# Edge attention: VectorE's one-hots and scalings take their second operand from PSUM instead of SBUF

## The reference, cut to what matters

```python
e = attn_src[:, src_idx] + attn_dst[:, dst_idx]
e = jnp.where(e >= 0, e, NEG_SLOPE * e)
e = e * edge_weight[None, :]
e_exp = jnp.exp(e - jnp.max(e))
denom = jax.ops.segment_sum(e_exp.T, dst_idx, num_segments=num_nodes).T
alpha = e_exp / (denom[:, dst_idx] + 1e-10)
msg = h[:, src_idx] * alpha[..., None]
out = jax.vmap(lambda m: jax.ops.segment_sum(m, dst_idx, num_segments=num_nodes))(msg)
```

## Time and profile before

| | us |
|---|---|
| median of 3 runs | 5927.24 |
| lowest and highest | 5904.29, 5947.91 |
| profiled execution, span | 5765.0 |
| TensorE, busy | 4607.2 (80%) |
| VectorE, busy | 2716.3 (47%) |
| ScalarE, busy | 2120.2 (37%) |
| GpSimd, busy | 836.5 (15%) |
| mean granted clock of TensorE | 0.885 |

### The profile page before, as it was taken

The page is one execution under the profiler, slowest core; times in us unless marked ns, Lnnn a source line. Parts: engine busy times, 40 slices in busy tenths (PEclk is TensorE's granted clock), DMA queues, the critical chain, the costliest instruction groups (busy, mean ns, idle before and its releaser), DMA issues. The chain is left out here.

```text
span 5765.0 us, 88635 instructions
## 1 busy us (share of the span) xinstructions
PE 4607.2 (80%) x24482; PEld 3873.4 (67%) x24483; DVE 2716.3 (47%) x5068; ACT 2120.2 (37%) x3279; POOL 836.5 (15%) x769
## 2 busy tenths in 40 slices
PE   3888868888856499669589989899769959969666
PEld 2677645555545399438578778788659959969555
DVE  5555567777653400321379689689631140020233
ACT  2333215544433200424256566566524420020332
POOL 2778710000005200002100000000022200000000
PEclk8788889999968799789799999999779979989878
DMA  3433311211113342113211111111122134224000
GB/s 97 113 111 106 101 37 71 79 71 75 66 62 100 106 161 109 30 34 116 65 51 56 46 44 55 42 49 55 39 71 97 36 93 162 109 92 159 36 17 24
DMA packets 150165, 438.52 MB, mean 76 GB/s; under 512 B 25592, under 2 KB 89805, under 8 KB 133676
## 3 DMA queue, kind: packets, MB, share of 16 engines
q1 hardware_dynamic: 115212, 341.23, 16.7%
q0 software_dynamic: 34848, 96.08, 5.9%
HBM read 340.98 MB, written 96.25 MB: 76 GB/s over the span
## 5 line engine op out<-in xcount | busy, mean ns | idle before, releaser
L2404 PE MATMUL p_acc<-p_H,p_eT 125*125 125x256 f32 x3750 | 823.5, 378 | 0.0
L2404 PEld LDWEIGHTS p_acc<-p_H,p_eT 125*125 125x125 f32 x3750 | 695.2, 187 | 106.0
L1033 POOL DMA_INDIRECT p_message<-edge_table,p_index x425 | 503.8, 1185 | 131.2 <-issue 120.9
L1951 DVE TENSOR_REDUCE p_mean<-F 128x1 f32<-128x3125 f32 x10 | 34.0, 3403 | 931.7 <-PEq L83 931.7
L1246 PE MATMUL p_acc<-p_message,p_spread 125*125 125x260 f32 x1666 | 425.6, 422 | 28.7 <-issue 28.7
L1298 POOL IOTA p_order_i<- 125x200 int32 x3 | 1.1, 381 | 2882.6 <-SPq L81 2882.6
L1705 ACT ACTIVATE p_hid<-p_up,p_b1s 128x125 f32<-128x125 f32 x764 | 273.0, 366 | 395.6 <-PE p_up L1681 352.5
L1246 PEld LDWEIGHTS p_acc<-p_message,p_spread 125*125 125x125 f32 x1666 | 348.4, 211 | 98.1 <-issue 30.6
L1681 PEld LDWEIGHTS p_up<-p_xT,p_w1s 128*128 128x128 f32 x3056 | 377.8, 199 | 51.3 <-issue 33.1
L1681 PE MATMUL p_up<-p_xT,p_w1s 128*128 128x125 f32 x3056 | 385.5, 283 | 32.9 <-issue 11.8
L835 PE MATMUL p_acc<-p_cell,p_heavy 125*125 (+1 forms) x1440 | 405.4, 392 | 0.0
(11 more groups left out here) (441 smaller groups left out, 8080.0 us busy)
## 6 DMA issues: line engine op xcount, KB each, us to landing
sums_first<-edge_sums SPq DMA_DIRECT2D x48, 1250.0 KB
p_second<-edge_sums SPq DMA_DIRECT2D x48, 1250.0 KB, 6.7
p_count<-edge_counts SPq DMA_DIRECT2D x75, 762.9 KB
edge_sums<-p_sums SPq DMA_DIRECT2D x32, 1250.0 KB, 4.4
edge_counts<-p_total SPq DMA_DIRECT2D x32, 610.4 KB
p_w1s<-in_L_ffn_W SPq DMA_DIRECT2D x16, 1024.0 KB
p_got<-made SPq DMA_DIRECT2D x25, 560.0 KB
p_dst_all<-dst_row SPq DMA_DIRECT2D x25, 531.2 KB
```

Of the source, the lines that this page charges most:

```text
L1033: pool.indirect_dma_start(message[:, m, k, :], None, table, bass.IndirectOffsetOnAxis(ap=index[:, m, k:k + 1], axis=0)).then_inc(landed[m] ...
L1951: then(dve.tensor_reduce(mean[:, h:h + 1], F[:, h], AX_X, ALU.add))
L2404: last = pe.matmul(acc[:, s, 0:C], eT[:, r % 4, a % 4], H[:, a, 0:C], start=(a == 0), stop=(a == T - 1))
```

## The change

Two tensors are added in PSUM. `dst_of` is a copy of `g.dstf` (443 columns), made once by ScalarE at the start. `power` holds the exponentials, 4 for each chunk; ScalarE writes them there by a second ACTIVATE in front of the one that writes them into `message` (TensorE still multiplies those columns, so that one stays). The comparison in `spreads` reads `dst_of` for `g.dstf`, and the product in `scales` reads `power` for the last columns of `message`. The wait in `scales` asks for both ACTIVATEs.

```diff
+        dst_of = ph.psum("dst_of", [P, 512])
+        power = ph.psum("power", [P, SETS, R_CH, HEADS])
+        dst_kept = ph.sem("dst_kept")
...
             def exponents(r, m):
                 act.wait_ge(logit_ready, r + 1)
+                act.activation(power[:, m], logit[:], ACT.Exp, bias=minus[:, m:m + 1]).then_inc(raised, 1)
                 act.activation(message[0:P, m, :, C:W], logit[:], ACT.Exp, bias=minus[:, m:m + 1]).then_inc(raised, 1)
...
             for m in range(SETS):
                 indices(m, m)
+            act.activation(dst_of[:, 0:CH + PAD], g.dstf[:], ACT.Copy).then_inc(dst_kept, 1)
             act.wait_ge(setup, 2)
...
                     dve.tensor_tensor(spread[:, lo:lo + n], g.iota[:, nodes(t)].unsqueeze(1).to_broadcast([P, n, P]),
-                                      g.dstf[:, bass.ds(r * R_CH + lo, n)].unsqueeze(2).to_broadcast([P, n, P]),
+                                      dst_of[:, bass.ds(r * R_CH + lo, n)].unsqueeze(2).to_broadcast([P, n, P]),
                                       ALU.is_equal).then_inc(spread_ready, 1)
...
-                dve.wait_ge(raised, r + 1)
+                dve.wait_ge(raised, 2 * r + 2)
                 for lo, n in PIECES:
                     rows_of = message[0:P, m, lo:lo + n]
                     o = rows_of[:, :, 0:C].rearrange("p k (h o) -> p k h o", h=HEADS)
-                    dve.tensor_tensor(o, o, rows_of[:, :, C:W].unsqueeze(3).to_broadcast([P, n, HEADS, HO]), ALU.mult).then_inc(scaled, 1)
+                    dve.tensor_tensor(o, o, power[:, m, lo:lo + n].unsqueeze(3).to_broadcast([P, n, HEADS, HO]), ALU.mult).then_inc(scaled, 1)
...
             (first, _, _), = g.tiles_of(nc, DVE, 0)
+            dve.wait_ge(dst_kept, 1)
             spreads(0, first, 0)
```

## The result

| | before | after |
|---|---|---|
| median, us | 5937.57 (4 runs) | 6128.39 (4 runs) |
| lowest and highest | 5904.29, 5955.75 | 6123.31, 6131.05 |
| profiled execution, span | 5765.0 | 6127.9 (timed at 6129.59) |

The ratio is 1.030, 95% interval 1.027 to 1.034: slower by 191 us, where 42 us less were forecast.

A forecast was written before the change was run, and what follows sets the result against it. GpSimd's gathers were taken to set the pace, 25.4 us a round, with TensorE's chain next at 23.4. Waits of 36.4 + 5.5 = 42 us go, added work costs 0: 5927 to 5885 us, range 5843 to 5935.

The forecast's parts named there:

- Gathers lose their stretch: GpSimd's 425 gathers beside one-hots and scalings: their stretch goes entirely, taking 102 us off GpSimd.
- The row it rested on: Line 1758 in another stage, one operand in PSUM: the gather beside it took 0.97 us; all six such pairs read so.
- The second operand in PSUM costs nothing: One-hots and scalings on VectorE: reading one operand from PSUM was taken as 0, with a lower bound of -11 ns an instruction.
- the rest of what was added: Second ACTIVATE, scalings' wait for two, later factors and the copy: hidden beside other work, cost 0; uncovered, the ACTIVATE costs 8.8 us.
- rival with a dear broadcast operand: One-hots and scalings cost more with a PSUM broadcast operand, VectorE becomes the bound: 5923 if doubled, 5993 at 2.5; chance 0.06.
- What of it reaches the end: Edge-attention stage: of 102 us off GpSimd only what TensorE now waits is gained, 42 us.
- the sum of the waits: Per round the smaller of VectorE's landing wait and TensorE's transpose wait: 36.4 us in rounds 3 to 24, plus 5.5 us.
- Does a new wait take their place? ... I count nothing: Refilled gathers land just in time behind a one-visit round, with 8 us to spare behind two; counted as nothing.
- TensorE's chain of 23.4 us: A two-visit round without gather waits: visits 17.47, terms 3.4, transpose to next visit 2.5 us; the next bound.
- The 162 us between span and median: Difference between the profiled span of 5765 and the median of 5927; expected to stay unchanged.
- The range: Whole-kernel median expected between 5843 and 5935 us, forecast plus runs' spread, third case and no effect partly included.
- the one rival on the slow side: Same as the rival with a dear broadcast operand: VectorE becomes the bound; chance 0.06.

The follow-up runs named there:

- extras only: The change with both operands read from SBUF again, all added work kept: 5747 us, 0.997 in one session; 5938 us, 1.000 in another.
- first chip: The chip of set 1, on which the kernel before took 5758 us; on the other four it took 5865 to 5938 us.
- Each half: Against the kernel before, only the one-hots (5718 us, 0.992) or only the scalings (5717 us, 0.992) read their second operand from PSUM.
- set 3: Another chip, against before: extras only 1.000, one-hots alone from PSUM 1.031, scalings alone from PSUM 1.001, before with a register load behind each gather 1.012.
- set 5: GpSimd waits for the new maximum: the change, before all 17 gathers 1.018, behind the first five 0.998; kernel before, behind the first five 0.989.
- sets 2 to 4: Runs on three other chips: the change again, register loads, halves, added comparisons behind the one-hots and 80-byte gathers; ratios to before from 1.000 to 1.041.
- paced kernels: A GpSimd register load added behind each gather: on the change 6011 us, 1.022; on the kernel before 5999 us, 1.012.
- held kernel: One-hots alone from PSUM, plus an unread comparison with both operands in SBUF behind each one-hot piece: 6031 us, 1.028.
- set 1: One chip: kernel before unchanged 5757 us, 1.000; extras only 0.997; one-hots alone from PSUM 0.992; scalings alone from PSUM 0.992.
- set 2: Another chip: kernel before unchanged 5862 us; the change again 6097 us, 1.038; the change with a register load behind each gather 6011 us, 1.022.

## Why the prediction was wrong, point by point

- **Gathers lose their stretch: right.** Forecast 950 ns, measured 946; 119 gathers ran beside the two lines, all at 0.95 us. The two lines are its cause: 1052 with the one, 1066 with the other. The row it rested on has more like it than was said: 46 gathers of that stage, and not six, overlap an instruction of line 1758; 45 took 0.97 or 0.98 us, one 1.08.
- **The second operand in PSUM costs nothing: right,** and so did the rest of what was added (extras only: 0.997 and 1.000). The rival with a dear broadcast operand fell: 1215 against 1217 ns.
- **What of it reaches the end: right only on the first chip.** Each half gave 40 us there, where I had put 42 for both, so the sum of the waits was hit by luck or was too small; the two together were not run there. The scalings' half gives nothing on the chip of set 3.
- **"Does a new wait take their place? ... I count nothing": this step failed.** I asked only whether the rows would land in time, and took TensorE's chain of 23.4 us as a length that GpSimd leaves alone. In the trace after, a round of two visits lasts 39.7 us (391.70 to 431.41 in the rows above): from the end of its visits to the transpose it is 16.4 us and not 3.4, and the maximum is read 3.2 us late. Before, GpSimd set the pace, and its gathers, 1.49 us apart on average, reached over the whole round, held up by every one-hot piece and scaling, so that most stretches without a hold were short. After, GpSimd is through in 21 us, waits for TensorE's last visit (430.1 us in 22 rounds), and then issues its next 17 right over terms and maximum, in most rounds anew. That this coincidence makes the loss is shown by set 5, where a wait that moves the gathers ends it; that the shorter gathers bring it about is read from the traces, and the sets 2 to 4 go with it: 7 to 11 late maxima where the time is that of before, 18 to 20 where it is 3 to 4% more (gathers of 946 to 965 ns), the paced kernels apart. The held kernel is the exception that isn't explained, with 1009 ns and 18.
- **"The 162 us between span and median": misread.** The profiled execution after was timed at 6129.59 us with a span of 6127.9, so next to nothing lies around a span. ("What lies around the first and last instruction", as I wrote above the prediction, was a guess.) By its stage (772.2 us to the last matmul, 771.8 in set 1, 873.1 in set 2) the trace of before is like that of the first chip, and its runs are like those of the others, where the kernel before had late updates of its own. The gap was the sign that something could disturb this program, and I took it for overhead.
- **The range** ended at 5935 us, and the one rival on the slow side was another mechanism.

Open: whether the change gains its 0.7% and more on a chip like the first; through what the gathers reach TensorE's sequencer and its updates, why that begins at the fifth gather of a run, and why one chip of five shows none of it. The making of descriptors, their number and their completions were not told apart.

## What to carry to other kernels

An engine that is taken off the bound does not only stop being late: ask when its next burst begins, and what serial handshake it will then lie over. Here long unbroken runs of indirect DMAs did least harm away from such a handshake, and one wait that parts them at it took the whole loss away, and gave 1.1% in the kernel before. And if the profiled span and the runs differ by more than a few us, find out why before any sum is made.

## What the runs showed of the hardware

- On four of five chips unbroken runs of GpSimd's indirect DMAs, 1.25 us apart, went with register instructions of TensorE at 0.7 us in place of 0.05 (and some of SyncE's, and of GpSimd's own in the two kernels with register loads), and with semaphore updates of TensorE that took effect late: in the kernel after the 17 late maxima were read 3.2 to 3.6 us after the end of the last gather of the run, and the worst, 19.1 us after its transpose, was one of the kernel before (457.61). In the kernel before of set 2 eight of 11 came while the run still went on. On the first chip the kernel before, the extras and both halves showed neither, with runs of up to 31 gathers that nothing held up.
- In the kernels with gathers of 946 to 965 ns and nothing that parts the runs, six traces, none of 3814 register instructions beside the first four gathers of a run was slow, and 1057 of 2772 from the fifth on.
- It does not depend on the bytes gathered: 80 or 1040 a row gave the same ratio, 1.041.
- A comparison or product of VectorE with both inputs in SBUF holds an indirect DMA of GpSimd up, 1.45 against 0.95 us beside one of 500 elements; with one input in PSUM it doesn't (119 gathers beside such instructions at 0.95 us), and takes as long as before (677 and 1215 against 682 and 1217 ns).
